# Attention in float32: the attended values as 64-column products, two heads side by side, all sixteen of a pair in one run

## The chip, the cores and the metric

The kernel runs on one core of a Trainium2 chip. Its time is the device time of one execution in microseconds (us); lower is better. Three runs of the kernel before took 1202.6, 1205.44 and 1205.76 us, so its median is 1205.44 us.

The engines that matter are PE (the matrix engine; PEld is its weight loads), DVE (the vector engine), ACT (the scalar engine), POOL (a second, slower vector engine) and SP, which issues most DMAs. Each works through its own list of instructions in the order in which they are written, and waits where a semaphore has not come far enough.

## The reference

The input is x of 4 x 512 x 256 in float32. Three layers add to it: half of a mixture of eight experts (two chosen per row), an attention, and half of the same mixture again. Only the attention is touched:

```
q  = rms_norm(x @ wq_a) @ wq_b          # 16 heads of 64 plain + 64 rotated columns
kv = rms_norm(x @ wkv_a part) @ wkv_b   # keys and values from 64 latent columns
attn = softmax(q k^T * scale)           # per batch and head 512 x 512
out  = attn @ v                         # 512 x 64 for each head
x    = x + out @ wo
```

`attn @ v` is the attended value of a head. All of it is float32, and the result has to be as good as float32 makes it.

## The kernel before, in words

The kernel has a first mixture, the projection of keys and latent values, the attention over 32 *pairs* (4 batches times 8 pairs of heads), the output projection and a second mixture. Key and value weights are folded into the query and output weights, so that the values of every head of a batch are the same 512 x 64 latent matrix.

A pair `p` has eight score tiles `k` = 0 to 7 of 128 queries by 512 keys. Each engine has its own list for a pair (`pair`, one per engine), and the lists of all pairs follow one another (`head_pairs`). For a tile the work goes round four engines:

- `scores` (PE, L1525 to L1527): three products of 512 columns into one of the banks 0 to 3. A float32 number is kept as a high part and a low part of the type float32r, and high times high, high times low and low times high are summed.
- `row_max` (DVE, L1184), then `exp` (ACT, L810) with its sum, into one of two buffers.
- `transposed` (PE, L1535): four 128 x 128 transposes into bank 4 or 5.
- `high_probs` (ACT, L819) and `low_probs` (DVE, L1214): the transposed tile is taken out as a high part and a low part.
- `attend` (PE, L1551, L1552): the product with the latent values, written to bank 6. Its stationary operand has 128 columns, 64 of high values beside 64 of low values or of zeros, so that half of bank 6 holds one part of the sum and half the other. There are 32 products of 256 columns in a pair, in eight pieces of four, one piece after the scores of each tile. `take_output` takes the halves out on ACT (L838) and DVE (L1208), and POOL adds them (L602).

PE issues the scores two tiles ahead of the transposes: in slot `k` of a pair its list has the transposes of tile `k`, then the scores of tile `k + 2` (tiles 8 and 9 are the first two of the next pair), then a piece of `attend`. DVE's list has in slot `k` the maximum of tile `k + 2`, then the low part of tile `k`; ACT's has the exponential of tile `k + 1`, then the high part of tile `k`.

Besides, each pair prepares the queries of the pairs that follow. PE makes three products into bank 7 (`queries`, L1514 and L1515: part 0 in slot 6, part 1 in slot 0, part 2 in slot 2). DVE turns two of them into rotated queries (`ropes`, L1191 and L1194), POOL adds these (L586), ACT takes the high parts of both kinds out (`queries_latent` L825 in slots 2 and 3, `queries_rope` L830 in slots 3 and 4), and DVE (L1199) and POOL (L595) the low ones. The first scores of the next pair, in slot 6, wait for both of POOL's low parts (`rope_low`). The inverse of the sums goes through a transpose of PE (L1558, slot 5), DRAM and a product on POOL (L610).

Of the kernel before, what the change touches and what calls it, by code (L numbers as in the profile page):

```python
# [20 lines left out]
F32 = mybir.dt.float32  # L21
# [7 lines left out]
P = 128  # L29
# [25 lines left out]
F32_SHARED = 13 * S + P  # L55
F32R_SHARED = 4 * GT * 3 * HD + 8 * S + 2 * GT * 2 * P + 2 * 3 * P
# [66 lines left out]
def build(nc, x_in, wq_a, qn_w, wq_b, wkv_a, kvn_w, wkv_b, wo, gate, w0, w1, wout, const, ids_in, out):  # L123
# [6 lines left out]
    with ctx:  # L130
# [128 lines left out]
        vh, vl = (split_area(wlo, 2 * B * S + k * B * GT * HD, [B, GT, HD]) for k in range(2))  # L259
# [9 lines left out]
        raw, rawl, inv, att = ([area((5 + 2 * n + k) * S, [S]) for k in range(2)] for n in range(4))  # L269
        invT = area(13 * S, [P], 8)  # L270
# [4 lines left out]
        pTh = [split_area(split, o + k * GT * 2 * P, [GT, 2 * P]) for k in range(2)]  # L275
        pTl = [split_area(parts, k * GT * 2 * P, [GT, 2 * P]) for k in range(2)]
        o += 2 * GT * 2 * P

        vcur = [split_area(split, o + par * 2 * GT * 3 * HD, [2, GT, 3 * HD]) for par in range(2)]
        o += 4 * GT * 3 * HD  # L280
        wch, wcl = (split_area(split, o + k * 3 * P, [3, P]) for k in range(2))
# [38 lines left out]
        k_high, k_low, v_split = sem("keys_high"), sem("keys_low"), sem("values_split")  # L320
# [4 lines left out]
        vcur_ready = sem("values_ready")  # L325
        s_psum, max_ready, exp_ready = sem("s_psum"), sem("max_ready"), sem("exp_ready")
        pT_psum, pT_high, pT_low = sem("pT_psum"), sem("pT_high"), sem("pT_low")
        o_psum, raw_sb, rawl_sb, raw_added = sem("o_psum"), sem("raw_sb"), sem("raw_low_sb"), sem("raw_added")
# [31 lines left out]
        def among(p, *these):  # L360

            return isinstance(p, int) and p in these

# [8 lines left out]
        def _(sp):  # L372
# [121 lines left out]
            sp.wait_ge(o_psum, NPAIR * 4)  # L494
# [18 lines left out]
        def _(pool):  # L513
# [47 lines left out]
            def load_weights(p, used):  # L561
# [5 lines left out]
                nc.gpsimd.tensor_copy(wch, src).then_inc(wc_high, 1)  # L567
                pool.wait_ge(wc_high, p + 1)
                pool.sem_inc(wc_low_due, 1)
                nc.gpsimd.tensor_tensor(wcl, src, wch.bitcast(F32), ALU.subtract).then_inc(wcur_ready, 1)  # L570
# [28 lines left out]
            def add_lower(p, par):  # L599
                pool.wait_ge(raw_sb, p * 2 + 2)  # L600
                pool.wait_ge(rawl_sb, p * 2 + 2)
                nc.gpsimd.tensor_tensor(raw[par], raw[par], rawl[par], ALU.add).then_inc(raw_added, 1)  # L602

            def multiply(p, par, fills, stored):
# [4 lines left out]
                pool.wait_ge(raw_added, p + 1)  # L609
# [4 lines left out]
            for par in range(2):  # L614
                for at in (0, 2 * HD):
                    last = nc.gpsimd.tensor_copy(vcur[par][:, 1, :, at:at + HD],
                                                 zrow[:, 0:HD].unsqueeze(1).to_broadcast([P, GT, HD]))
            last.then_inc(v_split, 1)
            load_weights(0, None)
# [4 lines left out]
            for g in range(NG):  # L624
# [3 lines left out]
                if g + 2 < NG:  # L628
# [3 lines left out]
                nc.gpsimd.tensor_copy(vh[:, g, :, :], keys[:, :, HD:2 * HD]).then_inc(v_split, 1)  # L632
                pool.wait_ge(v_split, g * 2 + 2)
                nc.gpsimd.tensor_tensor(vl[:, g, :, :], keys[:, :, HD:2 * HD], vh[:, g, :, :].bitcast(F32),
                                        ALU.subtract).then_inc(v_split, 1)
                if g == 0:
                    pool.wait_ge(v_split, 3)
                    load_values(0, 0, None)

            load_weights(1, 1)  # L640
# [3 lines left out]
            def pair(p, par, half):  # L644
# [6 lines left out]
                if not among(p, NPAIR - 2, NPAIR - 1):  # L651
                    load_weights(p + 2, p + 2)
                if not last:
                    rope_lower(p + 1, 1 - par)
                if not among(p, 0):
                    add_lower(p - 1, 1 - par)
                if not last:
                    load_values(p + 1, 1 - par, None if among(p, 0) else p * 4)
# [9 lines left out]
            add_lower(NPAIR - 1, 1)  # L668
# [17 lines left out]
        def _(act):  # L686
# [118 lines left out]
            def exp(s, k, par, first):  # L805

                act.wait_ge(max_ready, s + 1)
                if not first:
# [3 lines left out]
                                     accum_out=psum[par][:, k % 8:k % 8 + 1]).then_inc(exp_ready, 1)  # L812

            def high_probs(p, k, first):

                act.wait_ge(pT_psum, p * 8 + k + 1)
                if k % 2 == 0 and not (first and k < 4):
                    act.wait_ge(o_psum, p * 4 + k // 2 - 1)
                nc.scalar.copy(pTh[k // 2 % 2][:, :, (k % 2) * P:(k % 2 + 1) * P],  # L819
# [824 lines left out]
```

## Time and profile before

| what | value |
|---|---|
| median of 3 runs | 1205.44 us (1202.6 to 1205.76) |
| the profiled execution's own time | 1193.56 us |
| its span, first to last instruction | 1191.7 us |
| PE busy over the span | 1043.2 us (88%) |
| DVE busy | 824.7 us (69%) |
| ACT busy | 616.5 us (52%) |
| POOL busy | 502.7 us (42%) |
| granted PE clock, mean | 0.957 |

The profiled execution is 1.0% below the median of the timed runs, and 0.8% below the lowest. The shares are means over stages of different kinds: the attention over pairs lies between about 370 and 869 us. A matmul's duration in the profile reaches from its start until its result has left the array, so that the next one starts before it ends; what one costs the engine is the distance between two starts.

### The profile page before, as it was taken

How to read it: one execution, taken by the hardware profiler on the slowest of the kernel's cores; microseconds unless marked ns; L12 is line 12 of the kernel's file. 1: busy time of each engine (PE TensorE's matmuls, PEld its weight loads, DVE VectorE, ACT ScalarE, POOL GpSimd, SP SyncE). 2: the span in 40 equal slices, each digit the busy share in tenths (PEclk: the TensorE clock that was granted, in tenths of full speed). 3: DMA queues.
4: the chain of work that ended last, by engine and by line, in shares of the span. 5: the costliest groups of instructions: out<-in, count | busy, mean ns of one | idle time of the engine just before them, and what ended most of it. 6: DMA issues, size and time to landing. Idle time of an engine off the chain costs nothing.

```text
span 1191.7 us, 24657 instructions
## 1 busy us (share of the span) xinstructions
PE 1043.2 (88%) x6200; PEld 867.2 (73%) x6201; DVE 824.7 (69%) x1750; ACT 616.5 (52%) x1340; POOL 502.7 (42%) x464
## 2 busy tenths in 40 slices
PE   4579999995646999999999999999989729999995
PEld 4557888784634888888888888888778627887884
DVE  5365556643765999999999999999835455565552
ACT  1243334321125888888888888888810123343321
POOL 2542333333223555555555566655412532333332
PEclk9999999998677999999999999999999859999998
DMA  9844445332100011111010110011464463454231
GB/s 238 248 163 98 99 105 137 61 55 48 36 1 1 10 36 37 35 35 35 35 35 35 35 35 28 27 34 35 142 218 146 129 221 98 106 143 111 44 52 15
DMA packets 71562, 95.41 MB, mean 80 GB/s; under 512 B 9600, under 2 KB 48640, under 8 KB 71296
## 3 DMA queue, kind: packets, MB, share of 16 engines
q1 hardware_dynamic: 57216, 78.04, 21.3%
q0 software_dynamic: 14304, 16.87, 7.8%
q8 instruction: 19, 0.31, 0.1%
q14 instruction: 23, 0.19, 0.1%
HBM read 64.37 MB, written 34.43 MB: 83 GB/s over the span
## 4 chain that ended last, share of the span: by engine, by line
PE 47%; DMA 26%; issue 11%; DVE 4%; POOL 4%; ACT 1%; POOLq 1%; SPq 0%; DVEq 0%; ACTq 0%
DMA out<-shared,small 12%; DMA x_after_moe<-shared,small 12%; PE bank L1535 9%; PE bank L1551 7%; PE bank L1525 6%; PE bank L1552 5%; PE bank L1526 5%; PE bank L1527 5%; PE bank L1514 2%; POOL rows_by_expert L529 2%; PE bank L1515 2%; PE bank L1616 1%; PE bank L1476 1%; PE bank L1352 1%; PE bank L1354 1%
## 5 line engine op out<-in xcount | busy, mean ns | idle before, releaser
L810 ACT ACTIVATE shared<-bank,small 128x512 f32<-128x512 f32 x256 | 175.8, 687 | 57.9 <-DVE small L1184 55.5
L1184 DVE TENSOR_REDUCE small<-bank 128x1 f32<-128x512 f32 x256 | 175.2, 685 | 37.8 <-PE bank L1527 27.6
L1214 DVE TENSOR_TENSOR split_rows_and_inner<-bank,shared_split 128x512 fp32r<-128x512 f32 x256 | 174.7, 682 | 7.0 <-ACT shared_split L819 5.0
L762 ACT CAST split_rows_and_inner<-bank 128x512 fp32r<-128x512 f32 x78 | 45.7, 586 | 246.7 <-PE bank L1337 246.7
L1535 PE MATMUL bank<-constants,shared 128*128 128x128 f32 x1024 | 155.2, 274 | 0.9 <-ACT shared L810 0.9
L1551 PE MATMUL bank<-shared_split 128*128 128x256 f32 x512 | 144.4, 304 | 5.5 <-DVE shared L1208 2.2
L819 ACT CAST shared_split<-bank 128x512 fp32r<-128x512 f32 x256 | 147.3, 575 | 1.0 <-PE bank L1535 1.0
L1354 PE MATMUL bank<-expert_weights_low,split_rows_and_inner 128*128 x312 | 144.1, 462 | 0.0
L1356 PE MATMUL bank<-expert_weights_high,split_rows_and_inner 128*128 x312 | 143.0, 458 | 0.0
L1551 PEld LDWEIGHTS bank<-shared_split 128*128 128x128 f32 x512 | 96.3, 188 | 56.4 <-issue 27.3
L1552 PE MATMUL bank<-split_rows_and_inner,shared_split 128*128 128x256 f32 x512 | 132.8, 282 | 0.0
L1035 DVE TENSOR_TENSOR split_rows_and_inner<-bank,split_rows_and_inner 128x512 fp32r<-128x512 f32 x78 | 53.9, 690 | 113.5 <-ACT split_rows_and_inner L762 113.5
L1525 PE MATMUL bank<-expert_weights_high,shared_split 128*128 (+1 forms) x256 | 124.0, 484 | 6.4 <-POOL shared_split L595 6.4
L1352 PE MATMUL bank<-expert_weights_high,split_rows_and_inner 128*128 x312 | 125.5, 402 | 2.6 <-DVE split_rows_and_inner L1030 2.5
L542 POOL DMA_INDIRECT x_after_moe<-shared,small x39 | 60.9, 1561 | 150.2 <-DMA x_after_moe<-shared,small 120.5
L542 POOL DMA_INDIRECT out<-shared,small x39 | 60.5, 1552 | 150.5 <-DMA out<-shared,small 116.9
L1535 PEld LDWEIGHTS bank<-constants,shared 128*128 128x128 f32 x1024 | 118.1, 140 | 7.8 <-ACT shared L810 1.8
L595 POOL TENSOR_TENSOR shared_split<-shared,shared_split 64x512 fp32r<-64x512 f32 x64 | 82.0, 1281 | 56.3 <-ACT shared_split L830 56.2
L1526 PE MATMUL bank<-expert_weights_low,shared_split 128*128 (+1 forms) x256 | 102.1, 399 | 0.0
L1527 PE MATMUL bank<-expert_weights_high,shared_split 128*128 (+1 forms) x256 | 101.5, 397 | 0.0
L586 POOL TENSOR_TENSOR shared<-shared 128x512 f32<-128x512 f32 x32 | 41.0, 1281 | 142.0 <-DVE shared L1194 142.0
L1552 PEld LDWEIGHTS bank<-split_rows_and_inner,shared_split 128*128 128x128 f32 x512 | 96.6, 189 | 4.3
(191 smaller groups left out, 2483.8 us busy)
## 6 DMA issues: line engine op xcount, KB each, us to landing
expert_weights<-L_ffn_w_kernel SPq DMA_DIRECT2D x32, 512.0 KB, 4.6
shared<-rows_by_expert SPq DMA_DIRECT2D x78, 129.0 KB, 2.1
expert_weights<-L_ffn_wo_kernel SPq DMA_DIRECT2D x16, 512.0 KB, 6.1
shared<-inverse_sums SPq DMA_DIRECT2D x64, 128.0 KB, 2.9
attended_transposed<-shared SPq DMA_DIRECT2D x32, 256.0 KB, 2.7
expert_weights<-attended_transposed SPq DMA_DIRECT2D x2, 2048.0 KB, 10.2
shared<-attended_transposed SPq DMA_DIRECT2D x2, 2048.0 KB, 10.6
rows_by_expert<-empty_rows SPq DMA_DIRECT2D x23, 129.0 KB, 3.5
```

What stands on the lines that cost most here:

```text
L810: nc.scalar.activation(prob[k % 2], bank[k % 4][:, :], ACT.Exp, bias=negmax[:, k % 8:k % 8 + 1], accum_out=psum[par][:, k % 8:k % 8 + 1]). ...
L819: nc.scalar.copy(pTh[k // 2 % 2][:, :, (k % 2) * P:(k % 2 + 1) * P], bank[4 + k % 2][:, :].rearrange("p (c n) -> p c n", c=GT)).then_inc(p ...
L1184: V.tensor_reduce(negmax[:, k % 8:k % 8 + 1], bank[k % 4][:, :], AX.X, ALU.max, negate=True).then_inc(max_ready, 1)
L1214: V.tensor_tensor(pTl[k // 2 % 2][:, :, at], bank[4 + k % 2][:, :].rearrange("p (c n) -> p c n", c=GT), pTh[k // 2 % 2][:, :, at].bitcast( ...
L1354: mm(b[:, :], high, wlo[:, bass.ds(w, MLP)], start=False, stop=False)
L1356: last = mm(b[:, :], low, whi[:, bass.ds(w, MLP)], start=False, stop=(c == KC - 1))
L1525: mm(bank[k % 4][:, :], q_high, high, start=True, stop=False)
L1526: mm(bank[k % 4][:, :], q_high, low, start=False, stop=False)
L1527: mm(bank[k % 4][:, :], q_low, high, start=False, stop=True).then_inc(s_psum, 1)
L1535: last = tr(bank[4 + k % 2][:, c * P:(c + 1) * P], prob[k % 2][:, c * P:(c + 1) * P], ident)
L1551: mm(bank[6][:, at], vcur[par][:, 0, c, cols], pTh[half % 2][:, c, :], start=(c == 0), stop=False)
L1552: last = mm(bank[6][:, at], vcur[par][:, 1, c, cols], pTl[half % 2][:, c, :], start=False, stop=(c == GT - 1))
```

## The change

The 32 float32r products of a pair become 16 plain float32 ones. The stationary operand has 64 columns (the latent values, not split), and the two heads of a pair go to the two halves of bank 6, in turn, so that their products stand on different columns of the array. The probabilities are kept whole. They are copied out of banks 4 and 5 once for each tile, by ACT for the tiles 0, 4 and 7 and by DVE for the tiles 1, 2, 3, 5 and 6, to one of ten places. All sixteen products of a pair stand in one run in slot 1 of the next pair, behind the scores of tile 3. DVE takes bank 6 out with one copy; POOL's addition and ACT's two copies are gone. The tiles alternate between the two heads (`tile`), the query weights have two buffers instead of one, and the copies of the values for a pair are one on POOL instead of two.

```diff
+BY_ACT, BY_DVE = (0, 4, 7), (1, 2, 3, 5, 6)
...
+        def tile(k):
+            return k % 2, k // 2
+        def pT_place(par, k):
+            return k + 2 * par if k < 2 else k + 2
...
-                high, low = (src[:, bass.ds(p // PAIRS, 1), :, :] for src in (vh, vl))
-                nc.gpsimd.tensor_copy(vcur[par][:, :, :, HD:2 * HD], high.to_broadcast([P, 2, GT, HD]))
-                nc.gpsimd.tensor_copy(vcur[par][:, 0, :, :].rearrange("p t (n c) -> p t n c", n=3)[:, :, 0:3:2, :],
-                                      low.rearrange("p a t n -> p t a n").to_broadcast([P, GT, 2, HD])).then_inc(vcur_ready, 1)
+                nc.gpsimd.tensor_copy(vcur[par].unsqueeze(1), values[:, bass.ds(p // PAIRS, 1), :, :]).then_inc(vcur_ready, 1)
...
-                nc.gpsimd.tensor_tensor(raw[par], raw[par], rawl[par], ALU.add).then_inc(raw_added, 1)
...
-                nc.scalar.copy(pTh[k // 2 % 2][:, :, (k % 2) * P:(k % 2 + 1) * P],
-                               bank[4 + k % 2][:, :].rearrange("p (c n) -> p c n", c=GT)).then_inc(pT_high, 1)
+                nc.scalar.copy(pT[:, pT_place(par, k), :, :],
+                               bank[4 + k % 2][:, :].rearrange("p (c n) -> p c n", c=GT)).then_inc(pT_by_act, 1)
...
-                nc.scalar.copy(raw[par][rows_], bank[6][rows_, :]).then_inc(raw_sb, 1)
...
-            def take_output(p, par, hh):
+            def take_output(p, par):
+                dve.wait_ge(o_psum, p + 1)
+                if not among(p, 0, 1):
                     dve.wait_ge(att_ready, p - 1)
-                V.tensor_copy(rawl[par][rows_], bank[6][low_rows, :]).then_inc(rawl_sb, 1)
+                V.tensor_copy(raw[par], bank[6][:, :]).then_inc(raw_sb, 1)
...
-                V.tensor_tensor(pTl[k // 2 % 2][:, :, at], bank[4 + k % 2][:, :].rearrange("p (c n) -> p c n", c=GT),
-                                pTh[k // 2 % 2][:, :, at].bitcast(F32), ALU.subtract).then_inc(pT_low, 1)
+                V.tensor_copy(pT[:, pT_place(par, k), :, :],
+                              bank[4 + k % 2][:, :].rearrange("p (c n) -> p c n", c=GT)).then_inc(pT_by_dve, 1)
...
-                cols = slice((1 - hh) * HD, (1 - hh) * HD + P)
-                for c in (2 * piece, 2 * piece + 1):
-                    mm(bank[6][:, at], vcur[par][:, 0, c, cols], pTh[half % 2][:, c, :], start=(c == 0), stop=False)
-                    last = mm(bank[6][:, at], vcur[par][:, 1, c, cols], pTl[half % 2][:, c, :], start=False, stop=(c == GT - 1))
+            def attend(p, par):
+                pe.wait_ge(vcur_ready, p + 1)
+                pe.wait_ge(pT_by_act, (p + 1) * len(BY_ACT))
+                pe.wait_ge(pT_by_dve, (p + 1) * len(BY_DVE))
+                if not among(p, 0):
+                    pe.wait_ge(raw_sb, p)
+                for half in range(2):
+                    for c in range(GT):
+                        for hh in range(2):
+                            a, b = (pT_place(par, half * 4 + n * 2 + hh) for n in range(2))
+                            last = mm(bank[6][hh * HD:(hh + 1) * HD, half * 2 * P:(half + 1) * 2 * P].rearrange("p (t n) -> p t n", t=2),
+                                      vcur[par][:, c, :], pT[:, a:b + 1:b - a, c, :], start=(c == 0), stop=(c == GT - 1))
+                last.then_inc(o_psum, 1)
...
-                    if k > 1:
-                        attend(p, par, k // 2 - 1, k % 2, first)
-                    elif not first:
-                        attend(p - 1, 1 - par, 3, k)
+                    if k == 1 and not first:
+                        attend(p - 1, 1 - par)
```

PE's list in slot 1 and the start of slot 2 of a pair inside the loop. Before, with a piece of `attend` (L1551, L1552) after the scores of tile 3 (bank 3); L1535 are the transposes:

```order
L1535 MATMUL bank5<-constants,shared 128x128 x4
L1525 MATMUL bank3<-expert_weights_high,shared_split_49 128x512
L1526 MATMUL bank3<-expert_weights_low,shared_split_49 128x512
L1527 MATMUL bank3<-expert_weights_high,shared_split_49 128x512
L1551 MATMUL bank6<-shared_split_49 128x256
L1552 MATMUL bank6<-split_rows_and_inner,shared_split_49 128x256
L1551 MATMUL bank6<-shared_split_49 128x256
L1552 MATMUL bank6<-split_rows_and_inner,shared_split_49 128x256
L1535 MATMUL bank4<-constants,shared 128x128 x4
L1525 MATMUL bank0<-expert_weights_high,shared_split_49 128x512
```

The same place in the changed kernel, where the transposes are L1523, the scores L1511 to L1513 and the attended values L1537:

```order
L1523 MATMUL bank5<-constants,shared 128x128 x4
L1511 MATMUL bank3<-expert_weights_high,shared_split_49 128x512
L1512 MATMUL bank3<-expert_weights_low,shared_split_49 128x512
L1513 MATMUL bank3<-expert_weights_high,shared_split_49 128x512
L1537 MATMUL bank6<-shared 64x256 x16
L1523 MATMUL bank4<-constants,shared 128x128 x4
L1511 MATMUL bank0<-expert_weights_high,shared_split_49 128x512
```

In this slot sixteen products stand where four stood, and in the other seven slots none stands between the scores of a tile and the transposes of the next.

DVE's list in slots 2 and 3, before. L1208 is `take_output` of the second head, L1184 a maximum, L1214 a low part of probabilities, L1199 a low part of queries; ISA and REGISTER_ALU prepare the instruction that follows them:

```order
L1208 COPY shared<-bank6 64x512 [waits o_psum]
L1183 REGISTER_ALU
L1184 TENSOR_REDUCE small<-bank0 128x1 [waits s_psum]
L1214 TENSOR_TENSOR split_rows_and_inner<-bank4,shared_split_49 128x4x128 [waits pT_high]
L1198 ISA
L1199 TENSOR_TENSOR shared_split_49<-bank7,shared_split_49 64x512 [waits qz_high]
L1183 REGISTER_ALU
L1184 TENSOR_REDUCE small<-bank1 128x1 [waits s_psum]
L1214 TENSOR_TENSOR split_rows_and_inner<-bank5,shared_split_49 128x4x128 [waits pT_high]
```

And in the changed kernel, where `take_output` is L1192, the maximum L1169, the copy of probabilities L1201 and the low part of queries L1184:

```order
L1192 COPY shared<-bank6 128x512 [waits att_ready,o_psum]
L1168 REGISTER_ALU
L1169 TENSOR_REDUCE small<-bank0 128x1 [waits s_psum]
L1201 COPY shared<-bank4 128x512 [waits o_psum,pT_psum]
L1183 ISA
L1184 TENSOR_TENSOR shared_split_49<-bank7,shared_split_49 64x512 [waits qz_high]
L1168 REGISTER_ALU
L1169 TENSOR_REDUCE small<-bank1 128x1 [waits s_psum]
L1201 COPY shared<-bank5 128x512 [waits pT_psum]
```

The order here is the same. The wait at its head is for the whole run of sixteen products, no longer for one piece of four, and a copy waits for the transposes alone, no longer for ACT.

## Rows read from the trace of the kernel before

**Rows 1.** Thirty periods: us, then busy of PE, PEld, DVE, ACT, POOL; clock; DMA.
```profile
398.70:862.87 464.17, 460.04 (x2846) 377.97 (x2844) 427.53 (x687) 394.85 (x929) 264.37 (x265) 1.00 0.12 40
```
**Rows 2.** The transpose of the inverse sums: its line, and one row in time.
```profile
L1558 PE MATMUL bank<-constants,small x32: 269/272/274, 398.7 to 868.0; 128*8 128x128 f32 x32
...
862.87 0.27 PE L1558 MATMUL bank<-constants,small 128*8 128x128 f32 x1
```
**Rows 3.** Groups of DVE, 450 to 800 us: form, count | busy us, mean ns | idle before.
```profile
L1184 DVE TENSOR_REDUCE small<-bank 128x1 f32<-128x512 f32 x181 | 123.9, 684 | 20.2 <-PE bank L1527 12.6
...
L1208 DVE COPY shared<-bank 64x512 f32<-64x512 f32 x45 | 31.0, 688 | 1.4
L1194 DVE TENSOR_TENSOR shared<-bank,constants 128x512 f32<-128x512 f32 x23 | 15.7, 681 | 0.0
```
**Rows 4.** Groups of ACT, 450 to 800 us.
```profile
L810 ACT ACTIVATE shared<-bank,small 128x512 f32<-128x512 f32 x181 | 124.3, 687 | 37.1 <-DVE small L1184 35.4
L819 ACT CAST shared_split<-bank 128x512 fp32r<-128x512 f32 x180 | 103.6, 576 | 0.0
...
L830 ACT CAST shared_split<-shared 64x512 fp32r<-64x512 f32 x45 | 27.9, 621 | 0.5
L825 ACT CAST shared_split<-bank 64x512 fp32r<-64x512 f32 x46 | 26.7, 581 | 0.6
```
**Rows 5.** Chain that ended last, in order of time: start us, us, what.
```profile
562.27 0.44 PE bank L1535 x4
562.71 0.24 PE bank L1525
...
563.42 0.23 PE bank L1514
```
**Rows 6.** Instructions in order of time: start us, us, engine, line, operation.
```profile
561.40 0.40 PE L1527 MATMUL bank<-expert_weights_high,shared_split 128*128 x1
...
561.63 0.28 PE L1551 MATMUL bank<-shared_split 128*128 128x256 f32 x1
...
561.83 0.69 DVE L1184 TENSOR_REDUCE small<-bank 128x1 f32<-128x512 f32 x1 [0.24 <-PE bank L1527]
...
561.99 0.28 PE L1552 MATMUL bank<-split_rows_and_inner,shared_split 128*128 128x256 f32 x1
...
562.44 0.68 DVE L1214 TENSOR_TENSOR split_rows_and_inner<-bank,shared_split 128x512 fp32r<-128x512 f32 x1
...
563.15 0.68 DVE L1208 COPY shared<-bank 64x512 f32<-64x512 f32 x1
```
**Rows 7.** The same view, around the first scores of the next pair.
```profile
568.86 0.69 ACT L810 ACTIVATE shared<-bank,small 128x512 f32<-128x512 f32 x1
...
568.91 1.28 POOL L595 TENSOR_TENSOR shared_split<-shared,shared_split 64x512 fp32r<-64x512 f32 x1 [0.50 <-ACT shared_split L830]
...
569.69 0.66 PE L1535 MATMUL bank<-constants,shared 128*128 128x128 f32 x4
...
570.33 0.49 PE L1525 MATMUL bank<-expert_weights_high,shared_split 128*128 x1
...
570.90 0.39 PE L1527 MATMUL bank<-expert_weights_high,shared_split 128*128 x1
```
**Rows 8.** In order of time: plain float32 products of 256 columns, full array.
```profile
869.04 4.26 PE L1616 MATMUL bank<-value_out_weights,expert_weights 128*128 128x256 f32 x19
```
**Rows 9.** The same view: products with 64 stationary columns, heads on alternate halves.
```profile
71.74 2.77 PE L1461 MATMUL bank<-shared 64*64 64x256 f32 x12
```
**Rows 10.** Instructions by line: ns min/median/max, first and last start.
```profile
L1302 PE MATMUL bank<-gate_weights,value_out_weights x64: 349/361/381, 17.0 to 58.8; 128*128 128x8 f32 x64
...
L1302 PE MATMUL bank<-gate_weights,shared x64: 172/257/362, 892.5 to 952.9; 128*128 128x8 f32 x64
...
L1461 PE MATMUL bank<-shared x32: 630/631/632, 70.9 to 77.3; 64*64 64x256 f32 x32
...
L1616 PE MATMUL bank<-value_out_weights,expert_weights x128: 378/379/463, 869.0 to 921.8; 128*128 128x256 f32 x128
```

More of the change, by code:

```diff
@@ L268, in build @@
         ropeA, ropeB, rope = (area((2 + k) * S, [S]) for k in range(3))
-        raw, rawl, inv, att = ([area((5 + 2 * n + k) * S, [S]) for k in range(2)] for n in range(4))
-        invT = area(13 * S, [P], 8)
+        raw, inv, att = ([area((5 + 2 * n + k) * S, [S]) for k in range(2)] for n in range(3))
+        invT = area(11 * S, [P], 8)
         o = 0
@@ L274, in build @@
         o += 8 * S
[L275 to L281, printed above, removed]
+        pT = area(F32_SHARED + o, [10, GT, P])
+        o += PT_WORDS
+        values = area(F32_SHARED + o, [B, GT, HD])
+        o += B * GT * HD
+        vcur = [area(F32_SHARED + o + par * GT * HD, [GT, HD]) for par in range(2)]
+        o += 2 * GT * HD
+        wch, wcl = ([split_area(split, o + (2 * k + par) * 3 * P, [3, P]) for par in range(2)] for k in range(2))
         xTh, xTl = (split_area(parts, k * 3 * D, [3, KC, P]) for k in range(2))
@@ L613, in _ @@
             pool.wait_ge(wa_ready, 1)
[L614 to L619, printed above, removed]
+            load_weights(0, 0, None)
             for g in range(2):
@@ L651, in pair @@
                 if not among(p, NPAIR - 2, NPAIR - 1):
-                    load_weights(p + 2, p + 2)
+                    load_weights(p + 2, par, p + 1)
                 if not last:
                     rope_lower(p + 1, 1 - par)
[L655 to L658, printed above, removed]
+                    load_values(p + 1, 1 - par, None if among(p, 0) else p)
             for p in range(4):
@@ L805, in exp @@
             def exp(s, k, par, first):
+                hh, qt = tile(k % 8)
                 act.wait_ge(max_ready, s + 1)
@@ L848, in pair @@
                     s = p * 8 + k
-                    if k == 2 and not first:
-                        take_output(p - 1, 1 - par, 1)
-                    if k == 6:
-                        take_output(p, par, 0)
                     if not (last and k == 7):
                         exp(s + 1, k + 1, par if k < 7 else 1 - par, first and k < 1)
-                    high_probs(p, k, first)
+                    if k in BY_ACT:
+                        copy_pT(p, par, k)
                     if k in ((3, 4) if first else (2, 3)) and not last:
@@ L1501, in flat, with queries @@
                 return v.rearrange("p a n -> p (a n)")
-            def queries(p, part):
+            def queries(p, par, part):
                 src = flat(cq[:, bass.ds(p // PAIRS, 1), :])
@@ L1513, in queries @@
                     pe.wait_ge((ropeA_sb, ropeB_sb)[part - 1], p + 1)
-                mm(bank[7][:, :], wch[:, part, :], src, start=True, stop=False)
-                mm(bank[7][:, :], wcl[:, part, :], src, start=False, stop=True)\
+                mm(bank[7][:, :], wch[par][:, part, :], src, start=True, stop=False)
+                mm(bank[7][:, :], wcl[par][:, part, :], src, start=False, stop=True)\
                     .then_inc((qa_psum, qb_psum, qz_psum)[part], 1)
             def scores(p, par, k):
-                hh, qt = k // 4, k % 4
+                hh, qt = tile(k)
                 if k == 0:
@@ L1531, in transposed @@
                 pe.wait_ge(exp_ready, s + 1)
-                if not (first and k < 2):
-                    pe.wait_ge(pT_low, s - 1)
+                if k > 1:
+                    wait_pT(pe, p, k - 2)
+                elif not first:
+                    wait_pT(pe, p - 1, k + 6)
                 for c in range(GT):
@@ L1536, in transposed @@
                 last.then_inc(pT_psum, 1)
-            def attend(p, par, half, piece, first=False):
-                hh, at = half // 2, slice((half % 2) * 2 * P, (half % 2 + 1) * 2 * P)
-                if piece == 0:
-                    if half == 0:
-                        pe.wait_ge(vcur_ready, p + 1)
-                    pe.wait_ge(pT_low, p * 8 + half * 2 + 2)
-                    if half % 2 == 0 and not (first and half == 0):
-                        pe.wait_ge(raw_sb, p * 2 + hh)
-                        pe.wait_ge(rawl_sb, p * 2 + hh)
-                cols = slice((1 - hh) * HD, (1 - hh) * HD + P)
-                for c in (2 * piece, 2 * piece + 1):
-                    mm(bank[6][:, at], vcur[par][:, 0, c, cols], pTh[half % 2][:, c, :], start=(c == 0), stop=False)
-                    last = mm(bank[6][:, at], vcur[par][:, 1, c, cols], pTl[half % 2][:, c, :], start=False, stop=(c == GT - 1))
-                if piece == 1:
-                    last.then_inc(o_psum, 1)
+            def attend(p, par):
[11 more added lines that the diff above has]
+                last.then_inc(o_psum, 1)
             def inverse_transpose(p, par):
@@ L1593, in _ @@
             inverse_transpose(NPAIR - 1, 1)
-            for piece in range(2):
-                attend(NPAIR - 1, 1, 3, piece)
+            attend(NPAIR - 1, 1)
             def second_route(g, part):
```

99 lines of the change are left out of this document (44 added, 55 removed).

## The prediction

> **What bounds the kernel now.** I read the busy times of one long stretch first. Between the first and the thirty-first transpose of the inverse sums lie thirty periods, from 398.70 to 862.87 us [rows 2], which makes 15.47 us a pair; the reader is to see there that PE's busy time fills the stretch and that DVE has 427.53 of 464.17 us [rows 1]. PE's share says little, since its rows overlap, so I take the distances between its starts. The transposes of a tile take PE 0.44 us and its scores 0.71 [rows 5], a product of `queries` 0.23 (as L1527 to L1551, [rows 6]), and one of `attend` 0.12 (three steps from 561.63 to 561.99, [rows 6]). A pair then costs PE 8 x 1.15 + 6 x 0.23 + 32 x 0.12 + 0.1 = 14.5 us. DVE has 22 large operations in a pair: 8 maxima, 8 low parts, 2 halves of bank 6, 2 low parts of queries and 2 rotations. They take 0.68 to 0.69 us each [rows 3, 6], 15.0 in all; where nothing has to be prepared or waited for, two starts are only 0.61 apart (561.83 to 562.44), otherwise 0.71 (562.44 to 563.15) [rows 6]. PE and DVE are thus both nearly full, and DVE hardly waits: its largest idle time is 20.2 us before 181 maxima [rows 3], 0.1 us each.
>
> This works because of the order. From the last scores of tile k to the transposes of tile k, PE has a piece of `attend`, the transposes and scores of tile k + 1 and another piece: 0.48 + 1.15 + 0.48 = 2.1 us. The way round the other engines in that time is: scores out and seen by DVE (0.16 us after PE has moved on, since L1527 lasts 0.40 and the next starts after 0.23; then 0.03 to the maximum at 561.83) [rows 6], maximum 0.69, 0.04 us to ACT, and 0.83 from the start of the exponential to the transposes (568.86 to 569.69) [rows 7]. That is 1.75 us, so it fits.
>
> **The change, part by part, as engine sums.** DVE loses four operations (8 low parts and 2 halves become 5 copies and 1), 2.7 us a pair. ACT loses 5 of 8 copies of 0.58 [rows 4] and both halves of bank 6, 4.0 us. POOL loses an addition of 512 columns (L595, of half the rows, lasts 1.28, [rows 7]) and a copy. These copies exist in the trace in nearly the same form: the one of 64 rows on DVE lasts 0.69 and a product over 128 rows 0.68 [rows 3], so the number of rows costs nothing and I take 0.69.
>
> For PE, 32 products of 0.12 (3.8 us) give way to 16 in plain float32. Such a product is two rows in the trace. On the full array nineteen rows last 4.26 us [rows 8] and one 0.38 [rows 10], so they start (4.26 - 0.38)/18 = 0.216 us apart. With 64 stationary columns, and heads on alternate halves, twelve rows lasted 2.77 us [rows 9] at 0.63 for one [rows 10]. That stretch ran at the lower level of PE's clock (1.2 GHz): the granted clock is not lowered in the view, but rows of L1302 in it last 361 ns and later 257, and the same 256 columns take 0.63 there and 0.38 in L1616 [rows 10]. At that level single starts would be 0.43 apart and twelve rows would last 11 x 0.43 + 0.63 = 5.4 us; 2.77 is 5 x 0.43 + 0.63, six starts of two rows each. So two rows run side by side. At the full level a run of 32 rows is then 16 x 0.216 = 3.46 us. What the trace does not show is the same with 128 contracted rows (it had 64): the bound from the other side is 32 x 0.216 = 6.91. I take 3.46, as the nearest row says.
>
> The array has to change between 128 and 64 columns before and behind the run. No row of the attention shows it. At least it costs nothing; at most, as I see it, the last product has to leave first, 0.38 - 0.22 = 0.16 us [rows 10, 8]. I take 0.15 each way. The Trainium skill, "TensorEngine Tiling (Array Packing)", Key Properties, says that a change of the tiling mode (not of the tile alone) drains the engine. By it the sum below stands; without a drain the period is 0.3 shorter, 9 us over thirty.
>
> By sums PE would need 14.5 - 3.8 + 3.5 + 0.3 = 14.4 us, DVE 12.3, ACT less. But that is not how I cost it.
>
> **What the run in one place does.** Nothing now stands between the scores of one tile and the transposes of the next, so in a slot without a product of `queries` PE has 1.15 us where the way round needs 1.75: it waits. The run could give this back only if the others could work ahead in it. They can't: in the run DVE has the maximum of tile 3 and the copy of tile 1 left, and then stands at `take_output`, which waits for the run's end (the change's second pair of lists); ACT does exponential 3 and then stands at the queries of slot 2, whose product PE issues behind the run. So DVE's relief falls into the run, and the rest of its list stands outside it. I lay the latest waits of one period one behind another, from the end of the run:
>
> - drain 0.15, transposes 0.44, scores of tile 4 0.71, last products of `queries` 0.23 + 0.39, 0.05 to ACT: 1.97
> - ACT: latent part 0.58, exponential 0.69, latent part 0.58, rotated part 0.62, exponential 0.69, copy of tile 4 0.58, rotated part 0.62 [rows 4]: 4.36
> - POOL's second low part of the queries, 0.05, and 568.91 to 570.33 = 1.42 to the first scores of the next pair, which wait for it [rows 7]: 1.47
> - these scores until DVE's maximum, 570.33 to 571.29 and 0.03: 0.99
> - DVE: maximum 0.61, copy of tile 6 0.71, rotation 0.71, maximum 0.69: 2.72
> - exponential of tile 1 until its transposes, 0.04 + 0.83: 0.87
> - transposes and scores of tile 3: 1.15
> - drain 0.15 and the run 3.46: 3.61
>
> The sum is 17.14 us a period. Beside it, from the scores of tile 4, goes DVE's row of maximum 4, copy 2, low part, maximum 5, copy 3, low part, reciprocal, maximum 6; it reaches the transposes of tile 6 some 0.3 us before POOL does, so neither chain alone would shorten it much. The fill is thus 17.14 - 15.47 = +1.67 us in thirty periods, 50 us. The first pair has no run and gains about 1; at the end the run stands exposed (3.6 against a piece of 0.5), but the last pair has no scores left to issue: together +1. Parts that I cost at nothing: the second buffer of query weights and POOL's copies (hidden behind 200 us of POOL's idle time, 264 of 464 [rows 1]; if POOL were late, the first scores of a pair would be), and both mixtures.
>
> Against its own time of 1193.6 us the profiled execution would take 1244.6. The median of the timed runs is 11.8 us above it; on that basis the forecast is 1205.4 + 51.5, about **1257 us**. About 0.3% (3.6 us) is what a measurement can tell from no change.
>
> **Rivals.**
> - *No overlap with 128 contracted rows.* Each row has the array to itself, the run takes 6.91, and 31 runs add 107 us more: 1364. For it: the row of the trace has 64 rows only, and two streams must now be read over all partitions. Against it: in that row both heads read the same 64 partitions, so twice the stream from one partition did work. 7%.
> - *The run hides the waits, and the sums decide: faster.* Place: PE's wait for `exp_ready` before the transposes of tiles 4 to 7, 0 and 1. If DVE and ACT, with 3 and 4 us less to do, always deliver in time, PE's 14.4 us rule, 1.07 less in thirty periods, 32 us: 1173. It decides if the way round takes under 1.15 us, or if engines get well over one tile ahead in the run. For it: the relief is real, and DVE was as good as full. Against: 0.69 + 0.83 alone exceed 1.15. 10%.
> - *Between them.* A run of about 1.8 us (all four rows of two heads at once) would give a period of 15.5: no change, 1205. No row shows more than two at once. 3%.
> - *The forecast*, with run 3.46: 80%. Its own range is 1238 to 1278: no drains (-9), 0.3 us less for waits laid too long (-10), or 0.7 more for small gaps between twenty links (+20).
>
> The range for 8 in 10 reaches from 1228 to 1300. Faster has the chance 0.10, the same 0.03, slower 0.87.
>
> **What the profile after would show.** Starts of the transpose of the inverse sums 17.1 us apart. The rows of the run in twos, 16 starts of 0.216, 3.5 us in all, with the first transposes about 0.15 behind their place. DVE's idle time before `take_output` about 2 us a pair, and over 4 in all, with DVE at some 70% of the stretch; PE waiting 0.4 to 0.8 us for exponentials before transposes; the first scores of a pair waiting for POOL or just not. I am wrong if the run takes 7 us (first rival), or if PE stands at no exponential and the period is under 15.4 (second), or if DVE's copies are much shorter than 0.69.

## The result and the profile after

The changed kernel takes 1241.61 us (median of 4 runs, 1240.48 to 1242.52), the kernel before 1204.58 us beside it. The ratio is 1.031, with a 95% interval of 1.029 to 1.033: 3.1% or 37 us slower. The forecast was 1257 us, slower by 51.

The profiled execution took 1242.26 us. Cut at the same places as before, the view of busy time by stretch shows where the time went (columns as in [rows 1], x is the number of instructions):

```profile
0.00:377.66 377.66, 282.29 (x1608) 236.42 (x1609) 205.02 (x574) 110.90 (x200) 119.45 (x101) 0.93 0.40 102
377.66:405.56 27.90, 25.34 (x142) 18.17 (x143) 19.71 (x32) 16.90 (x40) 9.69 (x11) 0.96 0.00 1
405.56:909.55 503.99, 463.82 (x2846) 317.52 (x2844) 347.34 (x566) 294.99 (x717) 201.44 (x204) 1.00 0.11 37
909.55:916.29 6.74, 5.38 (x43) 3.56 (x41) 2.00 (x4) 2.15 (x7) 0.80 (x1) 1.00 0.30 89
916.29:1240.40 324.11, 272.91 (x1566) 229.31 (x1564) 162.43 (x447) 84.76 (x154) 99.92 (x77) 0.93 0.43 116
```

The third line is the thirty periods of [rows 1]: 503.99 us in place of 464.17, 16.80 us a pair in place of 15.47. That is +39.8 us. DVE has 80 us less to do in them than before and ACT 100, and the stretch is longer. In the kernel before, the other four lines read 372.06, 26.64, 6.17 and 322.66 us, so the whole attention (lines 2 to 4) takes 41.7 us more, 5 more than the 37 of the timed runs.

The 5.6 us more ahead of the attention belong to this execution or its chip, not to the change. They arise in the first mixture, where the DMAs moved less and PE did less in the same 60 us (before, then after; columns as in [rows 1]):

```profile
60.00:120.00 60.00, 50.58 (x316) 39.60 (x317) 36.13 (x103) 25.30 (x44) 20.03 (x17) 1.00 0.44 129
60.00:120.00 60.00, 42.58 (x270) 33.05 (x271) 29.01 (x95) 19.55 (x35) 16.95 (x16) 1.00 0.34 100
```

In the eight experiments below, which share this code with the changed kernel, the attention begins at 365.6 to 368.2 us, 4 to 6 us earlier than in the profile before. The change also takes work away there: POOL no longer splits the values into high and low parts. That this saves the 5 us by which the timed runs lie under the attention's 41.7 is likely but not shown, since the kernel before has one profile only.

One period in the order of time (start, duration, engine, line). L1537 are the attended values, L1523 the transposes, L1511 to L1513 the scores, L1500 and L1501 the products of the queries, L1192 the copy of bank 6, L822 and L827 the latent and rotated part of the queries on ACT, L607 POOL's low part. A bracket tells how long the engine was idle before, and on whom it waited; for PE it counts from the recorded end of the row before, about 0.16 us after PE could have gone on:

```profile
601.42 0.66 PE L1523 MATMUL bank<-constants,shared 128*128 128x128 f32 x4
601.53 0.69 DVE L1192 COPY shared<-bank 128x512 f32<-128x512 f32 x1 [2.33 <-PE bank L1537]
...
602.62 0.40 PE L1500 MATMUL bank<-expert_weights_high,shared_split 128*128 x1
602.82 0.69 DVE L1169 TENSOR_REDUCE small<-bank 128x1 f32<-128x512 f32 x1 [0.59 <-PE bank L1513]
...
603.28 0.58 ACT L822 CAST shared_split<-bank 64x512 fp32r<-64x512 f32 x1 [3.86 <-PE bank L1501]
...
604.80 0.65 PE L1523 MATMUL bank<-constants,shared 128*128 128x128 f32 x4 [0.42 <-ACT shared L805]
...
606.50 0.65 PE L1523 MATMUL bank<-constants,shared 128*128 128x128 f32 x4 [0.35 <-ACT shared L805]
...
607.56 1.28 POOL L607 TENSOR_TENSOR shared_split<-shared,shared_split 64x512 fp32r<-64x512 f32 x1 [0.56 <-ACT shared_split L827]
...
608.47 0.65 PE L1523 MATMUL bank<-constants,shared 128*128 128x128 f32 x4 [0.52 <-ACT shared L805]
...
608.97 0.49 PE L1511 MATMUL bank<-expert_weights_high,shared_split 128*128 x1
...
609.98 0.69 DVE L1169 TENSOR_REDUCE small<-bank 128x1 f32<-128x512 f32 x1 [0.80 <-PE bank L1513]
...
611.78 0.68 DVE L1169 TENSOR_REDUCE small<-bank 128x1 f32<-128x512 f32 x1
...
612.50 0.69 ACT L805 ACTIVATE shared<-bank,small 128x512 f32<-128x512 f32 x1 [0.54 <-DVE small L1169]
...
613.41 0.65 PE L1523 MATMUL bank<-constants,shared 128*128 128x128 f32 x4
...
614.37 0.39 PE L1513 MATMUL bank<-expert_weights_high,shared_split 128*128 x1
614.69 3.67 PE L1537 MATMUL bank<-shared 128*64 128x256 f32 x32
618.30 0.66 PE L1523 MATMUL bank<-constants,shared 128*128 128x128 f32 x4
```

The idle times in brackets tell it. When the run ends, DVE has been idle for 2.33 us and ACT, a little later, for 3.86; both wait for PE. In the rest of the period PE waits for exponentials before the transposes of tiles 4, 5 and 6 (0.42, 0.35, 0.52). The 32 rows of the run last 3.67 us. A row of it lasts 0.38 (min/median/max below), and they start in twos: two at 614.69, two at 614.96, then two every 0.216 us until 617.98.

```profile
L1537 PE MATMUL bank<-shared x1024: 379/379/431, 395.8 to 916.0; 128*64 128x256 f32 x171
```

Before, PE's matmuls had 1.1 us of waits in the thirty periods; the list of waits over them now has these among its longest (waiter, releaser: us in total, times, longest):

```profile
ACT shared_split L822 <- PE bank L1501: 111.9, 29, 3.9
...
DVE shared L1192 <- PE bank L1537: 70.9, 30, 2.4
...
PE bank L1523 <- ACT shared L805: 38.2, 90, 0.5
```

### The profile page after: what moved, and what is told of

Its sections match the earlier page's. It is cut to its first block, busy times and chain, and to the rows that moved or that the text cites. A ratio compares the mean times of both kernels' runs of the same rounds, so it can differ in the third digit from the quotient of the medians.

```text
span 1240.4 us, 23957 instructions
## 1 busy us (share of the span) xinstructions
PE 1049.7 (85%) x6200; PEld 805.0 (65%) x6201; DVE 736.5 (59%) x1622; ACT 509.7 (41%) x1116; POOL 431.3 (35%) x392
## 4 chain that ended last, share of the span: by engine, by line
PE 46%; DMA 19%; issue 15%; DVE 9%; ACT 5%; POOL 3%; SPq 1%; POOLq 0%; DVEq 0%; another core or an unknown queue 0%; ACTq 0%
DMA out<-shared,small 12%; PE bank L1523 10%; PE bank L1537 9%; DMA x_after_moe<-shared,small 5%; ACT shared L805 3%; PE bank L1511 3%; PE bank L1512 3%; PE bank L1513 3%; PE bank L1338 2%; DVE small L1169 2%; PE bank L1340 2%; DVE shared L1201 2%; PE bank L1342 2%; PE bank L1500 2%; PE bank L1501 2%
## 5 line engine op out<-in xcount | busy, mean ns | idle before, releaser
L1169 DVE TENSOR_REDUCE small<-bank 128x1 f32<-128x512 f32 x256 | 174.9, 683 | 94.5 <-PE bank L1513 93.6
L1523 PE MATMUL bank<-constants,shared 128*128 128x128 f32 x1024 | 164.0, 283 | 43.5 <-ACT shared L805 41.5
L1523 PEld LDWEIGHTS bank<-constants,shared 128*128 128x128 f32 x1024 | 112.8, 141 | 131.1 <-DVE shared L1201 55.3
L1340 PE MATMUL bank<-expert_weights_low,split_rows_and_inner 128*128 x312 | 144.2, 462 | 0.0
L1342 PE MATMUL bank<-expert_weights_high,split_rows_and_inner 128*128 x312 | 142.9, 458 | 0.0
L607 POOL TENSOR_TENSOR shared_split<-shared,shared_split 64x512 fp32r<-64x512 f32 x64 | 81.3, 1271 | 143.8 <-ACT shared_split L827 143.7
L1338 PE MATMUL bank<-expert_weights_high,split_rows_and_inner 128*128 x312 | 125.4, 402 | 3.5 <-DVE split_rows_and_inner L1015 3.3
L1511 PE MATMUL bank<-expert_weights_high,shared_split 128*128 (+1 forms) x256 | 124.2, 485 | 4.5 <-POOL shared_split L607 4.5
L1537 PE MATMUL bank<-shared 128*64 128x256 f32 x1024 | 117.6, 382 | 0.5 <-ACT shared L816 0.5
L1201 DVE COPY shared<-bank 128x512 f32<-128x512 f32 x160 | 108.8, 681 | 0.0
L1513 PE MATMUL bank<-expert_weights_high,shared_split 128*128 (+1 forms) x256 | 101.4, 396 | 0.0
L1537 PEld LDWEIGHTS bank<-shared 128*64 128x64 f32 x1024 | 71.1, 137 | 43.9 <-issue 12.0
L1350 PE MATMUL bank<-expert_weights_high,split_rows_and_inner 128*128 x312 | 90.7, 291 | 9.9 <-DVE split_rows_and_inner L1020 9.9
L1351 PE MATMUL bank<-expert_weights_low,split_rows_and_inner 128*128 x312 | 88.1, 282 | 0.0
L1352 PE MATMUL bank<-expert_weights_high,split_rows_and_inner 128*128 x312 | 88.1, 282 | 0.0
```

Source lines behind the costliest of these rows:

```text
L1169: V.tensor_reduce(negmax[:, k % 8:k % 8 + 1], bank[k % 4][:, :], AX.X, ALU.max, negate=True).then_inc(max_ready, 1)
L1201: V.tensor_copy(pT[:, pT_place(par, k), :, :], bank[4 + k % 2][:, :].rearrange("p (c n) -> p c n", c=GT)).then_inc(pT_by_dve, 1)
L1338: mm(b[:, :], high, whi[:, bass.ds(w, MLP)], start=(c == 0), stop=False)
L1340: mm(b[:, :], high, wlo[:, bass.ds(w, MLP)], start=False, stop=False)
L1342: last = mm(b[:, :], low, whi[:, bass.ds(w, MLP)], start=False, stop=(c == KC - 1))
L1511: mm(bank[k % 4][:, :], q_high, high, start=True, stop=False)
```

## The experiments

All of them are the changed kernel with one edit each. They ran in two groups, on two chips. Beside the first group (heads in groups of four, a quarter of the products, two runs in slots 1 and 5, four runs) the kernel before takes 1192.55 us, beside the second 1191.68, and not 1204.58 as above. So periods are compared first, and times as ratios to the kernel before. The period is read as for [rows 2]: the thirty-first start of the transpose of the inverse sums less the first, over thirty. By the ratio of 1.031 the changed kernel would take about 1229 us beside them (an estimate; it did not run there).

| kernel | first, 31st start | period us | time us | ratio to before (95%) |
|---|---|---|---|---|
| before | 398.70, 862.87 | 15.47 | | 1 |
| changed (other chip) | 405.56, 909.55 | 16.80 | 1241.61 | 1.031 (1.029 to 1.033) |
| heads in groups of four | 394.77, 929.50 | 17.82 | 1262.77 | one run |
| a quarter of the products | 391.84, 817.82 | 14.20 | 1146.52 | one run |
| both heads on one half | 398.48, 1005.62 | 20.24 | 1340.03 | one run |
| two runs, slots 1 and 5 | 393.31, 881.32 | 16.27 | 1210.50 | 1.015 (1.013 to 1.017) |
| four runs, slots 1, 3, 5, 7 | 394.39, 856.10 | 15.39 | 1184.75 | 0.993 (0.991 to 0.995) |
| one run, slot 4 | 394.71, 860.93 | 15.54 | 1193.43 | 1.002 (1.001 to 1.003) |
| two runs, slots 3 and 5 | 390.98, 852.55 | 15.39 | 1184.05 | 0.995 (0.993 to 0.996) |
| three runs, slots 3, 5, 7 | 391.38, 847.62 | 15.21 | 1179.77 | 0.991 (0.987 to 0.994) |

### Do the two heads run side by side?

```diff
                 for half in range(2):
-                    for c in range(GT):
-                        for hh in range(2):
+                    for hh in range(2):
+                        for c in range(GT):
```

> The run of sixteen products with the eight of one head first and then the eight of the other, so that neighbours never stand on different halves of the array; all else as in the changed kernel. If the two heads of the changed kernel run side by side (theory), each of the 32 rows now has the array to itself for 0.216 us: the run lasts 6.9 us in place of 3.5, a period grows from 16.8 to 20.2 us, and the time is about 1241.6 + 32 x 3.4 = 1350 us. If instead the two rows of one product run side by side (rival), the order of the heads does not matter: run 3.5 us, time 1241 us.

The edit was not quite what this text says: inside each half of the bank's columns it makes four products of one head and then four of the other, 4-4-4-4 and not 8-8. The run lasts 4.70 us, not 6.9:

```profile
616.21 4.70 PE L1537 MATMUL bank<-shared 128*64 128x256 f32 x32
620.84 0.66 PE L1523 MATMUL bank<-constants,shared 128*128 128x128 f32 x4
```

The period grew by 1.02 us and the run by 1.03 (4.70 - 3.67), so what the run gains goes wholly into the period. Neither side of the expectation was met: the order of the heads does matter, but neighbours of the same head don't cost the overlap altogether. Rows in flight in equal stretches of the run (columns: us, PE busy and rows in it, PEld busy and loads, clock, DMA) show how:

```profile
616.20:616.65 0.45, 0.44 (x2) 0.33 (x3) 1.00 0.00 0
616.65:617.10 0.45, 0.45 (x3) 0.27 (x2) 1.00 0.00 0
617.10:617.55 0.45, 0.45 (x5) 0.39 (x5) 1.00 0.00 0
617.55:618.00 0.45, 0.45 (x7) 0.33 (x3) 1.00 0.00 0
```

For 0.9 us the rows of the first head go one by one, then they overlap with rows of the other head, although these stand behind four products (eight rows) of the first in the list. Read row by row, the trace has starts at 616.21, 616.47, 616.69 and 616.90, then two together at 617.12 and 617.13: the fifth row of the first head and one more. To be sure that it is the halves of the array, both heads were put on the same one, in the same order of the loops:

```diff
-                            last = mm(bank[6][hh * HD:(hh + 1) * HD, half
+                            last = mm(bank[6][0:HD, half
```

> As the run with the heads in groups of four products, but both heads are written to the same half of bank 6, so all sixteen products stand on the same 64 columns of the array; head 0 is thereby left out of the result. If two rows run side by side only when they stand on different halves (theory), every row now waits for the one before: 32 x 0.216 = 6.9 us a run, period 16.8 + 3.4 = 20.2 us, 32 x 3.4 = 109 us more than the changed kernel. If the two rows of one product can run side by side (rival), the run stays at 4.5 us or less as with the heads in groups, period 17.8 us.

```profile
608.21 7.12 PE L1537 MATMUL bank<-shared 128*64 128x256 f32 x32
615.26 0.65 PE L1523 MATMUL bank<-constants,shared 128*128 128x128 f32 x4
```

31 starts of (7.12 - 0.38)/31 = 0.217 us: one at a time. The period is 20.24, as expected. Side by side is real, with 128 contracted rows too, and worth 3.45 us a pair.

This also tells what the second row at 617.13 was in the run before: not the sixth row of the first head, which can't start 0.01 us after the fifth on the same half. It was a row of the other head, and it went ahead of three rows listed before it.

### Does the run stand alone on the path?

```diff
-                    for c in range(GT):
+                    for c in range(1):
...
-                                      vcur[par][:, c, :], pT[:, a:b + 1:b - a, c, :], start=(c == 0), stop=(c == GT - 1))
+                                      vcur[par][:, c, :], pT[:, a:b + 1:b - a, c, :], start=True, stop=True)
```

> Of the sixteen products of a pair only four are made (one of the four chunks of keys), still in one run in slot 1; the rest of the sum is left out. Theory: the run stands alone on the path, so three quarters of 3.46 us go from every period: 16.8 - 2.6 = 14.2 us, and the time is about 1241.6 - 31 x 2.6 = 1161 us. Rival (the waits between tiles decide, and the other engines would use the run to get ahead): less than half of it comes back, period over 15.5, time over 1200 us. At 14.2 us the other engines' chain of maximum, exponential and transposes alone would be what is left, since PE's own work is then 11.6 us.

14.20 us a period, as the first theory had it, and 1146.5 us in all (15 less than said; the expectation had been reckoned from 1241.6, and from the estimate of 1229 it is 1229 - 31 x 2.6 = 1148). The run lasts 1.08 us in place of 3.67, 2.59 less, and the period is 2.60 shorter. The waits of PE for exponentials, 38.2 us in the changed kernel, are the same:

```profile
PE bank L1523 <- ACT shared L805: 38.2, 90, 0.5
ACT shared_split L822 <- PE bank L1501: 36.5, 29, 1.3
```

What shrank is ACT's idle time, from 111.9 to 36.5 us. So nothing was done ahead in the run.

### Place or number of pieces?

The bookkeeping for four of the next five is one edit: `attend` makes the chunks of keys that it is told, the semaphore of bank 6 counts halves (two a pair), and a table says which piece stands in which slot of PE's list.

```diff
+PIECES = {5: [(0, 0, (0, 1, 2, 3))], 1: [(1, 1, (0, 1, 2, 3))]}    # slot: (pairs back, half, chunks)
...
-                    if k == 1 and not first:
-                        attend(p - 1, 1 - par)
+                    for back, half, chunks in PIECES.get(k, ()):
+                        if back == 0:
+                            attend(p, par, half, chunks)
+                        elif not first:
+                            attend(p - 1, 1 - par, half, chunks)
```

> The eight products of the first four tiles move from slot 1 of the next pair to slot 5 of their own pair; the other eight stay in slot 1. Theory (the place of the run costs, since PE waits in slots without a filler): the run in slot 1 gets 1.73 us shorter; in slot 5 PE waited about 0.6 us before the transposes of tile 6, which the second run of 1.73 and two more changes of the array's columns (0.1 each) fill, so 0.6 us a period comes back: period 16.2 to 16.3 us, time about 1224 us, ratio to before 1.016. Rival (the products in this form cost by themselves, wherever they stand): the period does not fall, and with two more changes of columns it rises by 0.2: 1248 us.

Measured 16.27 us and a ratio of 1.015, as the first theory has it. PE's matmuls wait for exponentials 22.6 us in the thirty periods, in place of 38.2.

```diff
+PIECES = {5: [(0, 0, (0, 1))], 7: [(0, 0, (2, 3))], 1: [(1, 1, (0, 1))], 3: [(1, 1, (2, 3))]}
```

> Four runs of four products, in slots 5 and 7 of a pair and 1 and 3 of the next, the slots that have no product of the queries; bank 6 is taken out in slot 4. Theory: every slot of PE now has a filler of 0.46 or 0.86 + 0.2 us, the waits for exponentials go, and PE's own sum is left: 8 x 1.15 + 6 x 0.23 + 3.46 + 0.1 + 8 changes of columns x 0.1 = 14.9 us, with some waits 15.3; time about 1241.6 - 1.5 x 31 = 1195 us, a little faster than before. Rival (form of the products, changes of columns dear): 17 us a period or more, over 1245 us.

Measured 15.39 us and 0.993. PE's waits for exponentials were 38.2 us before matmuls and 13.2 before weight loads in the changed kernel. Of these this is left:

```profile
PEld bank L1526 <- ACT shared L806: 2.1, 7, 0.4
```

Each piece now costs PE more than its products. A run of four, and what stands before and behind it (L1516 the scores, L1544 the products, L1526 the transposes):

```profile
602.79 0.39 PE L1516 MATMUL bank<-expert_weights_high,shared_split 128*128 x1
...
603.11 1.08 PE L1544 MATMUL bank<-shared 128*64 128x256 f32 x8
...
604.12 0.66 PE L1526 MATMUL bank<-constants,shared 128*128 128x128 f32 x4
```

Without the change of columns the run would start at 602.79 + 0.23 and the transposes 0.86 later, at 603.88; they start at 604.12, so a run costs 0.24 us beside its products (0.09 ahead of it, 0.05 more between its first two starts than between the others, and 0.09 to 0.10 behind it).

Then the number was kept at one, and the place changed. With it, places were added for the probabilities, so the values lie elsewhere, and bank 6 is taken out in slot 5:

```diff
-                    if k == 1 and not first:
+                    if k == 4 and not first:
                         attend(p - 1, 1 - par)
...
-            return k + 2 * par if k < 2 else k + 2
+            return k + 5 * par if k < 5 else k + 5      # thirteen places for probabilities
```

> All sixteen products still in one run, but in slot 4 of the next pair in place of slot 1 (with thirteen places for the probabilities, so that no copy has to wait for it; bank 6 is taken out in slot 5). Theory: what costs is not the one piece but that slots 3 to 5 had no filler while the run stood beside slots that have a product of the queries. In slot 4 it covers the ways round to the transposes of tiles 5 and 6, whose waits (0.35 and 0.52 us) go; the other tiles have 1.15 + 0.46 = 1.61 us for a way of 1.75, so 0.15 each remains: PE's 14.4 us + 0.8 + a little: period 15.3 to 15.7 us, some 38 us faster than the changed kernel, ratio to before about 0.995 to 1.00. Rival (a run of 3.5 us in one piece starves DVE and ACT wherever it stands): period stays at 16.8 us, ratio 1.03.

15.54 us and 1.002 (1.001 to 1.003), the ratio a little over what was expected: the same 3.67 us in one piece, and 1.26 us a period come back by its place. DVE still stands idle for 2.27 us in it:

```profile
607.59 3.67 PE L1536 MATMUL bank<-shared 128*64 128x256 f32 x32
611.32 0.69 DVE L1191 COPY shared<-bank 128x512 f32<-128x512 f32 x1 [2.27 <-PE bank L1536]
```

What has gone is PE's waits for exponentials, 7.3 us in place of 38.2 in the thirty periods. That is 1.03 of the 1.26 us:

```profile
PE bank L1522 <- ACT shared L804: 7.3, 30, 0.3
```

So idle DVE is not the cost in itself; PE's waits are, and in slot 4 the run stands where PE waited before tiles 5 and 6.

```diff
+PIECES = {5: [(0, 0, (0, 1, 2, 3))], 3: [(1, 1, (0, 1, 2, 3))]}
```

> Two runs of eight products in slots 3 (second four tiles of the pair before) and 5 (first four tiles of the same pair), bank 6 taken out in slot 4. Against two runs in slots 1 and 5 (16.27 us a period) nothing differs but the place of one run. Theory: fillers beside slots 3, 4, 5 take the waits before tiles 4, 5, 6; PE 14.1 + 4 changes of columns x 0.13 + 0.15 x 5 = 15.4 us, ratio to before 0.99. Rival (number of pieces decides, not the place): 16.3 us, ratio 1.015.

15.39 us, 0.995. Against two runs in slots 1 and 5, moving one of them by two slots gives 0.88 us a period. The taking out of bank 6, which has to stand behind the run, moved along from slot 2 to slot 4 of DVE's list, so the edit is not of the place alone. But the waits of PE's matmuls for exponentials fell from 22.6 us to 0.9, which is 0.72 of the 0.88 us a period.

```diff
+PIECES = {5: [(0, 0, (0, 1))], 7: [(0, 0, (2, 3))], 3: [(1, 1, (0, 1, 2, 3))]}
```

> Three runs: eight products in slot 3, four in slot 5, four in slot 7; bank 6 taken out in slot 4. Against four runs (15.39 us a period) two changes of columns go (0.25 us), and slot 1 has no filler, which gives up to 0.3 us of waits before the transposes of tiles 2 and 3. Theory: 15.2 to 15.4 us, ratio to before 0.985 to 0.993. Rival (changes of columns cost nothing, waits all): 15.6 us or more.

15.21 us and 0.991. This version is faster than the kernel before, by 0.9% (0.6 to 1.3), and than the changed one by about 3.9% (0.991/1.031, two ratios from different chips). DVE and ACT now wait a lot, and PE hardly:

```profile
ACT shared L806 <- DVE small L1170: 124.4, 152, 1.6
DVE small L1170 <- PE bank L1516: 96.2, 122, 1.5
...
PEld bank L1526 <- issue: 42.8, 115, 0.5
```

No wait of PE's matmuls is among the twelve longest of that list. What bounds the period now is nearly PE's own row of instructions: 14.2 us by the prediction's sum without changes of columns, and 0.7 for three of them, of 15.21.

## Why the prediction was right

**What bounds.** That PE and DVE were both nearly full, and that sums of busy time would mislead, holds. The sums gave PE 14.4 us and DVE 12.3; the period became 16.8. What PE stood still, read from the distances between its starts in the period above, is 0.58, 0.51 and 0.67 us before tiles 4, 5 and 6, 0.25 and 0.12 before tiles 0 and 1, and 0.09 for POOL: 2.2 us, with which the sum of 14.4 comes within 0.2 of the period.

**The products.** Laid at 3.46 us for 16 starts of 0.216; measured 3.67 - 0.38 + 0.22 = 3.51. The overlap was read from a stretch with 64 contracted rows at the lower clock level and holds for 128 at the full one. That was the first rival's point (a run of 6.91 us), and the one-half experiment shows its price, 7.12 us and a period of 20.24.

**The run on the path.** Shown by the quarter of the products: 2.60 us of 2.59 come back.

**The waits without fillers.** Said: 0.4 to 0.8 us for exponentials. Measured: 0.42, 0.35 and 0.52 by the brackets. Of the second rival's claim, that DVE and ACT always deliver in time, nothing came true while the run stood in slot 1. What that rival had right is that PE's sum can rule: with the pieces placed where PE waited it nearly does, 15.2 us, of which 0.7 go into changes of the array's columns.

**The length of the chain.** The step that was mis-sized. The chain was laid at 17.14 us; between the two first transposes behind a run (601.42 and 618.30) lie 16.88, and the mean of thirty is 16.80. Link by link: DVE's four operations to the last maximum were put at 2.72, and are 609.98 to 612.46, 2.48, since the copy and the rotation follow one another after 0.60 us and not 0.71. ACT's seven operations were put at 4.36, and are 603.28 to 607.49, 4.21. The two drains were put at 0.15 each, and are 0.09 (614.37 + 0.23 to 614.69) and 0.10 (617.98 + 0.22 to 618.30). The others are within 0.1, some of them longer. With +1.33 in place of +1.67, thirty periods make 40 us, not 50. POOL was to be last by 0.3 us before the first scores of the next pair. It is last, but by less: these scores start 0.50 us after the transposes of tile 6 (608.47 and 608.97; 0.48 to 0.50 in all thirty periods) where other scores start after 0.41.

**The drain.** A gap of 0.09 and 0.10 us stands at the two ends of a run. The Trainium skill's rule that a change of the tiling mode drains the engine ("TensorEngine Tiling (Array Packing)", Key Properties) would give such gaps. This trace does not prove a full drain: the first row of the run starts 0.07 us before the recorded end of the scores' last row (614.69, and 614.37 + 0.39), and recorded ends of matmuls are modelled.

**The edges.** +1 us was said, with a gain in the first pair. The stretch before the first inverse transpose grew by 1.3 us, so that gain is not seen; that behind the last grew by 0.6, the rest of the execution by 1.5 behind it. They are single executions, so no more than that they are small is shown.

**The time.** The last step of the forecast did not carry over: it added 11.8 us because the median of the kernel before lay that far above its profiled execution. For the changed kernel the median lies 0.7 us below it (1241.61 and 1242.26). Of the 15 us between forecast and median, 12.5 come from this and 10 from the chain. The stretches outside the attention, 7.1 us longer and not forecast, and 0.8 more at the edges give 8 back. That the profiled execution came within 2.4 us of the 1244.6 laid for it is thus luck in part.

**The signs in the profile.** DVE at 69% of the stretch (70 said), idle 5.2 us a period (over 4 said), 2.33 of it before the copy of bank 6 (2 said).

## What to carry to other kernels

When two engines are both full, their list orders are part of the balance: a piece of work between a producer and the next consumer on PE was covering the way round the other engines, and moving it uncovers that way. Before a long piece is put anywhere, reckon for each wait what stands between the two ends of the round, in time, and put the piece where this is least; here the same 3.67 us cost 1.26 us a period less three slots further on. Relief of an engine counts only if it falls on the chain; in this change much of it became idle time beside the run (2.33 us of DVE, 3.86 of ACT).

## What the runs showed of the hardware

- Two float32 products of 64 stationary columns and 256 moving ones run side by side when they are written to different halves of the partitions: 32 rows in 3.67 us, against 7.12 on one half. Each product is two rows, and the pairing is that of rows.
- The partner need not be the neighbour in the list. With four products of a head in a row the overlap began after 0.9 us and 32 rows took 4.70 us. If a row could only start behind all rows listed before it, a group of eight could share just its last row with the next group, and 32 rows would take 29 starts, 6.3 us. The starts in the trace show it too: a row of the other half started at 617.13, with three rows listed before it still waiting for theirs.
- Going from 128 to 64 columns and back cost 0.1 us each way; with 0.05 more between the first two starts, a run costs 0.24 us beside its products.
- A copy from a PSUM bank on DVE took 0.68 us for 128 partitions as for 64 before (0.69, [rows 3]), with starts 0.60 apart.
